# A pre-norm block of relative-position attention and routed experts: routed rows sent from a copy, stores issued by SyncE, the residual's bias added a batch ahead

## The chip, the core and the metric

The kernel runs on one core of a Trainium2 chip. The metric is the device time of one execution in microseconds (us). Engines are named as in the profile: PE is TensorE, DVE is VectorE, ACT is ScalarE, POOL is GpSimd (Pool), SP is SyncE, which computes nothing and issues transfers.

## The reference

The input x has 8 batches of 1024 tokens of 128 features. One layer computes, in float32:

```python
x = x + attention(layernorm(x))   # own layernorm again inside; 8 heads of 16
#   content = (q + u) k^T ; pos = rel_shift((q + v) (pe Wp)^T)
#   score = (content + pos) / sqrt(128); ctx = softmax(score) v; ctx Wo + bo
x = x + ffn(layernorm(x))
#   router: h = gelu(layernorm(x Wr1 + br1)); probabilities of 8 experts, the best 2, renormalised
#   each expert: (x1 * gelu(x2)) W2 + b2, with x1, x2 = split(x W1 + b1); weighted sum of the two
```

The relative shift makes the position term of score[q, k] one form below the diagonal and another above it, so a head's scores are made from two sets of stacked operands.

## The kernel before

The attention phase is one loop over the 8 batches, `b`, unrolled inside over 8 heads `h` and 9 units `u` (unit 0 makes the diagonal blocks of the upper form, units 1 to 8 the blocks of 128 keys, kb = u - 1). The expert phase follows it. The order of all work in the loop is written out by hand: tables such as `SCATTER_AT` hold pairs (h, u), and each engine does the piece at the end of its part of that unit. Engines run in program order, and semaphores are all that ties them.

In each unit PE makes a half of the scores of head h in `pB` (second pass, L639 to L645), and a piece of the first pass of head h + 2 in `pA` (L618 to L624), whose row maxima DVE takes (L1008, L1014); then again. ACT takes the exponential of `pB` into one of four buffers `prob` (L921, L923). Pool masks it: it sets one element to zero (L516), cuts the lower triangle (L518) and adds the upper form (L523), which releases `p_mask`; in unit 0 it masks the whole diagonal (L511). PE multiplies masked blocks with the values `vext` into `pC` (L657), in four column strips side by side, two kb at a time, in units 4, 6 and 8 and, for the last two, in unit 1 of the next head (`PAIRS_AT`). `vext` has 16 values and a one for each head, padded to VW = 32 columns.

Between these each engine has pieces for other batches. For the next batch: projections, the rotation of positions on Pool in eight pieces (`positions`, L429 to L441, at `POSITIONS_AT`), the split of the operands in a high and a low part (`high` on ACT, `low` on DVE, L995), and their stores to DRAM (`store`, L443, on Pool's queue, at `STORE_AT`, two transfers of 512 KB each call, ten in a batch). SP loads them as stacks of a head (`stack`, L270), three heads ahead; the first head of the next batch waits until all are stored (semaphore `stored`, in head 5). SP also moves the row of maxima of the next head (L277), swaps pairs of partitions (`swap`, L262) and shifts the values (`vsh` from `held`, L332). For the batch before: `xres`, loaded in head 0 (L312), gets its bias from Pool (`residual`, L455, at (1, 1)), then the attention's output from DVE (`final`, L1055), is stored, and the router works on it: statistics, `root` on Pool (L463, L465), rows (`router_apply`, L1078, L1081), hidden layer, logits, the two best, places (L1146 to L1170). Then Pool sends each row of 132 numbers to its two places in `routed_rows`, 16 indirect transfers of 128 rows each (`scatter`, L467, L476, at `SCATTER_AT`): the first in head 7, 15 in the next round's heads 0 to 2. `router_apply` waits for them before it overwrites `rows`.

After the loop the last batch has its own tail: the residual, 15 scatters left of the batch before, the two roots and 16 scatters on Pool; the output, the router and the table of tiles on DVE. Then come the experts, 72 tiles of 256 rows.

## Time and profile before

| | us |
|---|---|
| median of 3 runs (lowest, highest) | 1770.41 (1769.01, 1772.16) |
| the profiled execution | 1768.02 |
| its span, first to last instruction | 1766.4 |
| busy: PE, DVE, POOL, ACT | 1576.1, 1432.4, 1156.7, 1089.7 |

The profile is a page on one execution and a trace that can be asked. A row of instructions gives the line, the engine, the tile written and those read, the shape and the count, then busy time and the mean of one, then the engine's idle time just before them and what ended it. A row by stretch gives its ends and length in us, then the busy time (and the count) of PE, its weight loads (PEld), DVE, ACT and POOL, then the granted clock as a share of 2.4 GHz, the busy share of the 16 DMA engines and GB/s. A row of a timeline gives start and duration in us, and in brackets the idle time before it with its releaser. The time falls into a start (to 104 us), the eight batches (to 1280 us), a tail (to 1368 us) and the experts.

### The profile page before, as it was taken

To read this page: it belongs to the slowest core of one execution; us is meant where nothing else is said; L and a number is where in the kernel's file an instruction comes from. 1 tells how busy PE (TensorE), PEld (TensorE's weight loads), DVE (VectorE), ACT (ScalarE), POOL (GpSimd) and SP (SyncE) were. 2 spreads that over 40 slices of the span, in tenths; PEclk is the share of its full clock that TensorE was granted. 3 is DMA by queue.
4 is the path that set the end of the run, shared out by engine and by line. 5 is a ranking of instruction groups with operands and counts; after the bars stand their busy time and mean duration, and the time that the engine had idled before them with its cause. 6 is when DMAs were issued, how large, how long until landed. Compare 5 with 4: busy or idle time off the path is not lost. (4 is left out here: it accounts for less than half of the span.)

```text
span 1766.4 us, 50630 instructions
## 1 busy us (share of the span) xinstructions
PE 1576.1 (89%) x12534; PEld 1235.8 (70%) x12535; DVE 1432.4 (81%) x5423; ACT 1089.7 (62%) x2143; POOL 1156.7 (65%) x2139
## 2 busy tenths in 40 slices
PE   2699999999999999999999999999930999999997
PEld 1466776677677677667767667766720899999997
DVE  3479989998998898899899889889943677777775
ACT  2136676666767667666676766766710666676665
POOL 4149759858856865975885686597553366666655
PEclk8569999999999999999999999999965999999999
DMA  4534733733644463373364446337361233333333
GB/s 161 168 103 102 184 93 101 185 104 108 158 111 130 108 181 89 99 187 103 105 167 107 129 109 182 87 108 179 96 191 57 43 50 53 48 52 51 50 53 42
DMA packets 140439, 195.85 MB, mean 111 GB/s; under 512 B 27976, under 2 KB 102616, under 8 KB 140192
## 3 DMA queue, kind: packets, MB, share of 16 engines
q1 hardware_dynamic: 92608, 130.86, 27.0%
q0 software_dynamic: 47584, 62.19, 17.6%
q8 instruction: 94, 1.54, 0.4%
q14 instruction: 153, 1.25, 0.2%
HBM read 108.24 MB, written 75.27 MB: 104 GB/s over the span
## 5 line engine op out<-in xcount | busy, mean ns | idle before, releaser
L1008 DVE CUSTOM_DVE_ANT_0 junk<-pA,lmask 128x512 bf16<-128x512 f32 x1056 | 691.5, 682 | 106.8 <-PE pA L620 57.3
L921 ACT ACTIVATE prob<-pB 128x512 f32<-128x512 f32 x384 | 229.5, 598 | 189.9 <-PE pB L639 114.6
L1487 POOL DMA_INDIRECT out<-yb,dst x144 | 232.9, 1617 | 163.4 <-ACT yb L1561 87.2
L618 PE MATMUL pA<-K,QL 96*128 96x512 f32 (+3 forms) x792 | 286.2, 363 | 1.6 <-DVE acc L1008 1.6
L641 PE MATMUL pB<-QL,K 97*128 97x512 f32 (+3 forms) x768 | 281.3, 366 | 0.0
L639 PE MATMUL pB<-QU,K 97*128 97x512 f32 (+3 forms) x640 | 264.7, 414 | 0.9
L657 PE MATMUL pC<-prob,vext 128*32 128x256 f32 x3088 | 221.2, 387 | 26.7 <-POOL prob L523 26.7
L620 PE MATMUL pA<-K,QU 96*128 96x512 f32 (+3 forms) x660 | 233.7, 355 | 4.0 <-DVE acc L1008 3.8
L923 ACT ACTIVATE prob<-pB 128x512 f32<-128x512 f32 x384 | 227.8, 593 | 0.4
L523 POOL TENSOR_TENSOR prob<-prob,upper_diag 128x128 f32<-128x128 f32 x384 | 190.8, 497 | 32.3
L476 POOL DMA_INDIRECT routed_rows<-rows_r,idx x159 | 165.1, 1038 | 49.3 <-issue 26.5
L639 PEld LDWEIGHTS pB<-QU,K 97*128 97x128 f32 x640 | 121.6, 190 | 79.2 <-issue 50.8
L1599 DVE SCALAR_TENSOR_TENSOR g<-pLin,b_all,gl 128x256 f32<-128x256 f32 x292 | 126.2, 479 | 55.1 <-PE pLin L1510 33.5
L618 PEld LDWEIGHTS pA<-K,QL 96*128 96x128 f32 x792 | 154.8, 195 | 19.2 <-DVE acc L1008 11.4
L657 PEld LDWEIGHTS pC<-prob,vext 128*32 128x32 f32 x3088 | 84.0, 110 | 113.6 <-POOL prob L523 42.5
L641 PEld LDWEIGHTS pB<-QL,K 97*128 97x128 f32 x768 | 146.7, 191 | 14.7 <-ACT upper_diag L921 0.4
L1554 ACT ACTIVATE gl<-pGate,b_all 128x256 f32<-128x256 f32 x292 | 122.5, 471 | 46.8 <-issue 36.3
L620 PEld LDWEIGHTS pA<-K,QU 96*128 96x128 f32 x660 | 130.2, 197 | 19.2 <-DVE acc L1008 9.0
L1516 PE MATMUL pY<-w_all,g 128*128 x1152 | 140.4, 275 | 0.0
L511 POOL TENSOR_SCALAR_AFFINE_SELECT upper_diag<-upper_diag 128x1024 f32<-128x1024 f32 x64 | 70.2, 1097 | 100.7 <-ACT upper_diag L923 99.8
L1516 PEld LDWEIGHTS pY<-w_all,g 128*128 128x128 f32 x1152 | 134.2, 192 | 0.0
L921 ACT ACTIVATE b_all<-pB 128x512 f32<-128x512 f32 x128 | 76.5, 598 | 83.8 <-PE pB L639 57.0
(305 smaller groups left out, 3696.1 us busy)
## 6 DMA issues: line engine op xcount, KB each, us to landing
QL<-split_operands SPq DMA_DIRECT2D x67, 256.0 KB, 3.4
QU<-split_operands SPq DMA_DIRECT2D x67, 256.0 KB, 3.9
K<-split_operands SPq DMA_DIRECT2D x67, 256.0 KB, 4.6
xg<-routed_rows SPq DMA_DIRECT2D x76, 132.0 KB
QL<-split_operands SPq DMA_DIRECT2D x67, 128.0 KB, 3.4
QU<-split_operands SPq DMA_DIRECT2D x67, 128.0 KB, 3.7
K<-split_operands SPq DMA_DIRECT2D x67, 128.0 KB, 3.8
split_operands<-c_h POOLq DMA_DIRECT2D x16, 512.0 KB, 7.3
```

What stands on the lines that cost most here:

```text
L476: po.indirect_dma_start(dram["xs"], bass.IndirectOffsetOnAxis(idx[:, t, j:j + 1], 0), rows[:, t, :], None).then_inc(scattered, 16)
L523: po.tensor_tensor(p, p, upper_diag[h % 2][:, P * kb:P * kb + P], ALU.add).then_inc(p_mask, 1)
L618: mm = pe.matmul(dst[:, 0:low], QL[0:KROWS, s, q], K[0:KROWS, s, k0:k0 + low], start=True, stop=True)
L620: mm = pe.matmul(dst[:, low:HALF], QU[0:KROWS, s, q], K[0:KROWS, s, k0 + low:k0 + HALF], start=True, stop=True)
L639: mm = pe.matmul(pB[:, q0:q0 + up], K[0:r, s, k], QU[0:r, s, q0:q0 + up], start=True, stop=True)
L641: mm = pe.matmul(pB[:, q0 + up:q0 + HALF], K[0:r, s, k], QL[0:r, s, q0 + up:q0 + HALF], start=True, stop=True)
L657: mm = pe.matmul(pC[VW * strip:VW * strip + VW, :], vext[:, kb, h % H, :], prob[kb % RING][:, quarter * strip:quarter * strip + quarter], ...
L921: act.activation(p[:, 0:HALF], pB[:, 0:HALF], ACT.Exp, scale=SCALE).then_inc(p_exp, 1)
L923: act.activation(p[:, HALF:S], pB[:, HALF:S], ACT.Exp, scale=SCALE).then_inc(p_exp, 1)
L1008: v.tensor_tensor_reduce(junk[:, n % S1_BUFS, :], pA[n % S1_BUFS][:, :], lmask[:, at:at + HALF], 1.0, -3.0e38, ALU.add, ALU.max, acc[:, s, ...
L1487: po.indirect_dma_start(dram["out"], bass.IndirectOffsetOnAxis(dst[k][:, a:a + 1], 0), yb[k][:, a, :], None, compute_op=ALU.add).then_inc( ...
L1516: mm = pe.matmul(pY[k % 2][:, a, :], g[k % 2][:, c, P * a:P * a + P], keep["w2"][:, bass.ds(ex * F + c * E, E)], start=(c == 0), stop=(c = ...
```

## The change

It adds two tiles, `sent` and `sent_to`. At the end of head 7 SP waits until the places of the round are written and the scatters of this round have landed, and copies `rows` and `idx` into them; all 16 scatters of these go out in the next round, spread over heads 0, 1 and 3 to 6, and the last batch's go out of `rows` directly. `router_apply` waits for the copy where it waited for the scatters. The operands' stores are issued by SP, in heads 2, 3 and 4, each behind a row of maxima. `xres` is loaded in head 5 for the next round, and its bias is added in two halves in head 7; the first is loaded and done in the start. The rotation's pieces move to heads 1 and 2, the last two stay. `vext` is 17 wide, and so are the strips of `pC`; the product that once fills `pC` ahead of the loop takes its weights from `ident`. Counts of semaphores follow (`SET_R` 15, `res_done` 2 a batch).

```diff
-        vext = sb("vext", [P, NB, H, VW])
+        vext = sb("vext", [P, NB, H, D + 1])
...
+        sent, sent_to = sb("sent", [P, NB, ROW]), sb("sent_to", [P, NB, TOPK], U32)
...
-        POSITIONS_AT = ((2, 1), (2, 2), (2, 4), (2, 5), (2, 6), (2, 8), (5, 4), (5, 6))
+        POSITIONS_AT = ((1, 1), (1, 4), (1, 8), (2, 1), (2, 4), (2, 6), (5, 4), (5, 6))
...
-        RSTD_AT = ((3, 2), (3, 4), (3, 6), (3, 7), (4, 0), (4, 1), (4, 2))
-        RESIDUAL_AT, LAST_HEADS_AT, FIRST_HEADS_AT = (1, 1), (0, 6), (6, 4)
+        RSTD_AT = ((3, 2), (3, 4), (3, 5), (3, 7), (4, 0), (4, 1), (4, 2))
+        RESIDUAL_AT, LAST_HEADS_AT, FIRST_HEADS_AT = ((7, 1), (7, 4)), (0, 6), (6, 4)
...
-        SCATTER_AT = ((7, 6), (0, 2), (0, 3), (0, 4), (0, 5), (0, 6), (0, 8), (1, 0), (1, 2), (1, 3), (1, 4), (1, 5), (1, 6), (1, 7), (1, 8), (2, 0))
-        SAME_ROUND = sum(h == H - 1 for h, _ in SCATTER_AT)
+        SCATTER_AT = ((0, 1), (0, 4), (0, 6), (0, 8), (1, 6), (3, 1), (3, 6), (3, 8), (4, 4), (4, 6), (5, 1), (5, 8), (6, 1), (6, 4), (6, 6), (6, 8))
...
-        STORE_AT = {(3, 1): ("c", 0), (3, 3): ("c", 1), (3, 5): ("k", 0), (4, 5): ("gl", 0), (4, 6): ("gu", 0)}
+        STORE_AT = {2: ("c",), 3: ("k",), 4: ("gl", "gu")}
...
+            def store(nb, name):
+
+                highs, lows = known(sp, nb * HI_N + READY[name]), known(sp, nb * LOW_N + READY[name])
+                sp.wait_ge(set_dve, DVE_SET)
+                sp.wait_ge(hi_done, highs)
+                sp.wait_ge(low_done, lows)
+                for op, row in PLACES[name]:
+                    for low in range(2):
+                        sp.dma_start(stored_to(nb, op, low, row), parts[name][low][:, :].bitcast(F32)).then_inc(stored, 16)
...
+            sp.dma_start(xres[:, :, :], dram["x"][B - 1].rearrange("(t p) e -> p t e", p=P)).then_inc(d_res, 16)
...
-                        sp.wait_ge(d_x2, written)
-                        sp.dma_start(xres[:, :, :], dram["x"][bass.ds((b + B - 1) % B, 1)].rearrange("o (t p) e -> p (o t) e", p=P)).then_inc(d_res, 16)
...
+                    for name in STORE_AT.get(h, ()):
+                        store(b + 1, name)
...
+                        written, applied = known(sp, b * 16 + 32), known(sp, (b + 1) * RLN_N)
+                        sp.wait_ge(set_dve, DVE_SET)
+                        sp.wait_ge(d_x2, written)
+                        sp.wait_ge(r_ln, applied)
+                        sp.dma_start(xres[:, :, :], dram["x"][bass.ds(b, 1)].rearrange("o (t p) e -> p (o t) e", p=P)).then_inc(d_res, 16)
+                    if h + 1 == H:
+                        placed_rows, all_sent = known(sp, (b + 1) * RPOS_N), known(sp, (b + 1) * SCAT_N)
+                        sp.wait_ge(set_dve, DVE_SET)
+                        sp.wait_ge(r_pos, placed_rows)
+                        sp.wait_ge(scattered, all_sent)
+                        sp.dma_start(sent[:, :, :], rows[:, :, :]).then_inc(copied_out, 16)
+                        sp.dma_start(sent_to[:, :, :], idx[:, :, :]).then_inc(copied_out, 16)
...
-            sp.wait_ge(d_x2, (B + 1) * 16)
-            sp.dma_start(xres[:, :, :], dram["x"][B - 1].rearrange("(t p) e -> p t e", p=P)).then_inc(d_res, 16)
...
-            def store(nb, name, place):
-
-                highs, lows = known(po, nb * HI_N + READY[name]), known(po, nb * LOW_N + READY[name])
-                po.wait_ge(set_pool, POOL_SET)
-                po.wait_ge(hi_done, highs)
-                po.wait_ge(low_done, lows)
-                op, row = PLACES[name][place]
-                for low in range(2):
-                    po.dma_start(stored_to(nb, op, low, row), parts[name][low][:, :].bitcast(F32)).then_inc(stored, 16)
-
-            def residual(b):
-                po.wait_ge(d_res, b * 16 + 16)
-                po.tensor_tensor(xres[:, :, :], xres[:, :, :], bo_rows[:, :].unsqueeze(1).to_broadcast([P, NB, E]), ALU.add).then_inc(res_done, 1)
+            def residual(b, half):
+                if half == 0:
+                    po.wait_ge(d_res, b * 16 + 16)
+                four = slice(4 * half, 4 * half + 4)
+                po.tensor_tensor(xres[:, four, :], xres[:, four, :], bo_rows[:, :].unsqueeze(1).to_broadcast([P, 4, E]), ALU.add).then_inc(res_done, 1)
...
-                    placed_rows = known(po, (b + 1) * RPOS_N)
+                    copies = known(po, b * 32 + 32)
                     po.wait_ge(set_r, SET_R)
-                    po.wait_ge(r_pos, placed_rows)
-                elif n == SAME_ROUND:
-                    po.wait_ge(set_r, SET_R)
+                    po.wait_ge(copied_out, copies)
+                    po.sem_inc(going_out, 1)
+                po.indirect_dma_start(dram["xs"], bass.IndirectOffsetOnAxis(sent_to[:, t, j:j + 1], 0), sent[:, t, :], None).then_inc(scattered, 16)
...
+            po.wait_ge(m_done, 1)
+            for half in range(2):
+                residual(0, half)
...
-            residual(B)
-            for n in range(SAME_ROUND, NB * TOPK):
-                scatter(B - 1, n)
+            for n in range(NB * TOPK):
...
-                    mm = pe.matmul(pC[VW * strip:VW * strip + VW, :], vext[:, kb, h % H, :], prob[kb % RING][:, quarter * strip:quarter * strip + quarter],
+                    mm = pe.matmul(pC[VW * strip:VW * strip + D + 1, :], vext[:, kb, h % H, :], prob[kb % RING][:, quarter * strip:quarter * strip + quarter],
...
-                    v.wait_ge(scattered, b * SCAT_N + SCAT_N - 16 * SAME_ROUND)
+                    v.wait_ge(copied_out, b * 32 + 32)
...
```

## Rows read from the trace of the kernel before

**Rows 1.** Busy time by engine, stretches near heads 0 to 3 and 5, fourth batch.
```profile
547.00:565.00 18.00, 16.98 (x138) 12.24 (x137) 16.34 (x55) 12.64 (x25) 13.24 (x24) 1.00 0.35 100
565.00:585.00 20.00, 18.27 (x154) 13.17 (x154) 16.86 (x74) 11.88 (x23) 17.37 (x34) 1.00 0.33 98
585.00:603.00 18.00, 16.59 (x132) 11.30 (x132) 16.74 (x66) 12.04 (x23) 16.74 (x31) 1.00 0.36 107
603.00:623.00 20.00, 18.54 (x147) 13.22 (x148) 18.39 (x71) 13.72 (x27) 18.21 (x44) 1.00 0.77 184
...
641.00:658.00 17.00, 16.05 (x136) 11.43 (x136) 16.38 (x66) 12.80 (x24) 11.96 (x27) 1.00 0.53 151
```
**Rows 2.** The page's groups by cost: busy us, mean ns | idle before.
```profile
L657 PE MATMUL pC<-prob,vext 128*32 128x256 f32 x3088 | 221.2, 387 | 26.7 <-POOL prob L523 26.7
...
L476 POOL DMA_INDIRECT routed_rows<-rows_r,idx x159 | 165.1, 1038 | 49.3 <-issue 26.5
```
**Rows 3.** Timeline of PE in head 1 of the fourth batch.
```profile
574.86 0.64 PE L657 MATMUL pC<-prob,vext 128*32 128x256 f32 x8 [1.32 <-POOL prob L523]
```
**Rows 4.** Timeline of POOL ahead of that product.
```profile
571.00 2.99 POOL L455 TENSOR_TENSOR xres<-xres,bo_rows 128x1024 f32<-128x1024 f32 x1
...
574.35 0.46 POOL L523 TENSOR_TENSOR prob<-prob,upper_diag 128x128 f32<-128x128 f32 x1
```
**Rows 5.** Line 451, Pool's stores: ns min/median/max, first and last start.
```profile
L451 POOL DMA_DIRECT2D split_operands<-k_h x8: 657/657/657, 178.4 to 1206.8; - x8
```
**Rows 6.** Timeline of ACT, the first exponential of batches 2, 3 and 4.
```profile
253.75 0.60 ACT L921 ACTIVATE upper_diag<-pB 128x512 f32<-128x512 f32 x1 [0.19 <-PE pB L645]
400.12 0.60 ACT L921 ACTIVATE upper_diag<-pB 128x512 f32<-128x512 f32 x1 [0.19 <-PE pB L645]
547.19 0.60 ACT L921 ACTIVATE upper_diag<-pB 128x512 f32<-128x512 f32 x1 [0.19 <-PE pB L645]
```
**Rows 7.** Busy time by stretch, as rows 1: one with a lower clock.
```profile
416.00:424.00 8.00, 7.18 (x40) 5.18 (x44) 5.49 (x27) 2.97 (x6) 6.57 (x12) 0.57 0.82 237
```
**Rows 8.** The same for stores of Pool (343) and of SP (52).
```profile
343.00:350.00 7.00, 7.00 (x68) 5.23 (x67) 6.89 (x43) 4.80 (x11) 6.00 (x13) 1.00 0.91 211
52.00:58.00 6.00, 0.00 (x0) 0.00 (x0) 0.11 (x2) 0.00 (x0) 4.55 (x9) 0.50 0.51 210
```
**Rows 9.** Timelines of SP and PE, second batch; the page's landing of K's loads.
```profile
353.56 1.19 SPq L270 DMA_DIRECT2D QL<-split_operands  x2
...
364.21 0.27 PE L618 MATMUL pA<-K,QL 96*128 96x128 f32 x1
...
K<-split_operands SPq DMA_DIRECT2D x67, 256.0 KB, 4.6
```
**Rows 10.** DVE's last router step, Pool's mask of (0, 1), and vsh's landing (line 332).
```profile
392.32 0.17 DVE L1170 TENSOR_TENSOR rows_r<-gd,rows_r 128x8 f32<-128x8 f32 x1
...
403.57 0.46 POOL L523 TENSOR_TENSOR b_all<-b_all,upper_diag 128x128 f32<-128x128 f32 x1 [0.17 <-POOL b_all L518]
...
DMA to landing us min/median/max: 8.4/9.7/11.2
```
**Rows 11.** Weight loads of lines 657 and 598: ns min/median/max, first and last start.
```profile
L657 PEld LDWEIGHTS pC<-prob,vext x3088: 106/110/177, 108.2 to 1281.8; 128*32 128x32 f32 x193
...
L598 PEld LDWEIGHTS pM<-ident_f,mneg x41: 82/83/92, 98.0 to 1269.4; 128*8 128x8 f32 x41
```
**Rows 12.** Timeline of SP in the start: the swap.
```profile
27.71 5.27 SPq L262 DMA_DIRECT2D rq<-rp  x2
```
**Rows 13.** Timelines of POOL and DVE in the tail.
```profile
1281.64 2.36 POOL L455 TENSOR_TENSOR xres<-xres,bo_rows 128x1024 f32<-128x1024 f32 x1
...
1303.67 0.28 POOL L463 TENSOR_SCALAR rs_r<-mv_r 128x8 f32<-128x8 f32 x1
1304.04 1.68 POOL L465 TENSOR_TENSOR rs_r<-rs_r,mhalf 128x8 f32<-128x8 f32 x1
...
1306.50 0.17 DVE L1078 TENSOR_SCALAR rows_r<-rows_r 128x8 f32<-128x8 f32 x1 [9.72 <-DMA routed_rows<-rows_r,idx]
```

More of the change, by code:

```diff
@@ L211, in attention_phase @@
         RHID_N, RTOP_N, RTOP_DLT, RPOS_N = 3 * NB, 2 * NB + 5, 2 * NB + 1, 8
-        D_R, SET_R = 16 * 3, 14
+        D_R, SET_R = 16 * 3, 15
         M_PRO, M_N, W_N = 5, len(M_AT), len(W_AT)
@@ L303, in _ @@
             sp.sem_inc(moved, 16)
+            sp.sem_inc(copied_out, 32)
             with batches(nc, sp) as b:
@@ L306, in _ @@
                     if h == 0:
-                        written, normed = known(sp, b * 16 + 16), known(sp, (b + 2) * LN_N)
+                        normed = known(sp, (b + 2) * LN_N)
                         sp.wait_ge(set_dve, DVE_SET)
@@ L470, in scatter, with scatter_last @@
                 if n == 0:
-                    placed_rows = known(po, (b + 1) * RPOS_N)
+                    copies = known(po, b * 32 + 32)
                     po.wait_ge(set_r, SET_R)
-                    po.wait_ge(r_pos, placed_rows)
-                elif n == SAME_ROUND:
-                    po.wait_ge(set_r, SET_R)
+                    po.wait_ge(copied_out, copies)
+                    po.sem_inc(going_out, 1)
+                po.indirect_dma_start(dram["xs"], bass.IndirectOffsetOnAxis(sent_to[:, t, j:j + 1], 0), sent[:, t, :], None).then_inc(scattered, 16)
+            def scatter_last(n):
+                t, j = divmod(n, TOPK)
+                if n == 0:
+                    po.wait_ge(r_pos, (B + 1) * RPOS_N)
                 po.indirect_dma_start(dram["xs"], bass.IndirectOffsetOnAxis(idx[:, t, j:j + 1], 0), rows[:, t, :], None).then_inc(scattered, 16)
@@ L489, in _ @@
             po.memset(rows[:, :, :], 0.0).then_inc(set_r, 1)
+            po.memset(sent[:, :, :], 0.0).then_inc(set_r, 1)
             po.memset(both[:, :, :], 0.0).then_inc(set_r, 1)
@@ L523, in _ @@
                             po.tensor_tensor(p, p, upper_diag[h % 2][:, P * kb:P * kb + P], ALU.add).then_inc(p_mask, 1)
-                        if (h, u) == RESIDUAL_AT:
-                            residual(b)
+                        if (h, u) in RESIDUAL_AT:
+                            residual(b + 1, RESIDUAL_AT.index((h, u)))
                         if (h, u) in RSTD_AT:
@@ L529, in _ @@
                             positions(b + 1, POSITIONS_AT.index((h, u)))
-                        if (h, u) in STORE_AT:
-                            store(b + 1, *STORE_AT[h, u])
                         if (h, u) == ROOT_AT:
@@ L537, in _ @@
                             scatter(b, SCATTER_AT.index((h, u)))
-            residual(B)
-            for n in range(SAME_ROUND, NB * TOPK):
-                scatter(B - 1, n)
+            for n in range(NB * TOPK):
+                scatter(B, n)
             for i in range(2):
@@ L543, in _ @@
             for n in range(NB * TOPK):
-                scatter(B, n)
-            po.wait_ge(scattered, B * SCAT_N + (2 * NB * TOPK - SAME_ROUND) * 16)
+                scatter_last(n)
+            po.wait_ge(scattered, (B + 2) * SCAT_N)
         @block.tensor
@@ L770, in _ @@
             for j in range(0, P, VW):
-                pe.matmul(pC[j:j + VW, :], vext[:, 0, H - 1, :], prob[1][:, 0:S // STRIPS], start=True, stop=False, skip_group_check=True)
+                pe.matmul(pC[j:j + VW, :], ident[:, 0:VW], prob[1][:, 0:S // STRIPS], start=True, stop=False, skip_group_check=True)
             with batches(nc, pe, 0) as b:
@@ L1190, in small_piece @@
                     if which == 0:
-                        v.wait_ge(res_done, b + 1)
+                        v.wait_ge(res_done, 2 * b + 2)
                     final(which, src, done)
@@ L1232, in _ @@
             v.tensor_copy(mrow[0][:, :], pM[0:NB, 0:P]).then_inc(m_done, 1)
-            v.wait_ge(set_r, 12)
-            v.tensor_copy(idx[:, :, :].rearrange("p t j -> p (t j)"), lane[:, :]).then_inc(set_r, 1)
+            v.wait_ge(set_r, 13)
+            v.tensor_copy(sent_to[:, :, :].rearrange("p t j -> p (t j)"), lane[:, :]).then_inc(set_r, 1)
             v.wait_ge(d_r, D_R)
@@ L1280, in _ @@
                 normalized(B, i)
-            v.wait_ge(res_done, B + 1)
+            v.wait_ge(res_done, 2 * B + 2)
             v.memset(padrow, 0.0).then_inc(set_pad, 1)
```

6 lines of the change are left out of this document (4 added, 2 removed).

## The prediction

> **What bounds the kernel now.** I read the page's list of groups first, then the busy time by stage of one typical batch (the fourth, 547 to 694 us), then who waited for whom, then the order of Pool's and TensorE's work around each wait. Eight batches fill 104 to 1280 us, 146.4 us from one start to the next [rows 6]; before them stands a start that transfers bound, behind them a tail and 400 us of experts, which the change does not touch. TensorE is the bound in the batches: head 5 takes 17 us with 16.05 busy [rows 1]. In heads 0 to 3 it is not alone. Of 76 us there it is busy for 16.98 + 18.27 + 16.59 + 18.54 = 70.4, so 5.6 are idle; VectorE is busy for 16.34 + 16.86 + 16.74 + 18.39 = 68.3, a close second [rows 1]. The page says what TensorE lacks: its context product pC waits 26.7 us in all for L523, the last of Pool's three masking steps [rows 2]. The longest case in a batch is 1.32 us at 574.86 [rows 3]. Pool's own order tells why: at 571.00 it adds the output bias over 128x1024 in one piece of 2.99 us, and the mask that this product lacks starts only behind it, at 574.35 [rows 4]; all through heads 0 and 1 scatters stand between the masks in the same way. Pool is late and not overloaded: in head 5 it is busy for 11.96 of 17 us, in head 1 for 17.37 of 20 [rows 1].
>
> **The change part by part.**
>
> *Scatters, stores, bias and rotations leave heads 0 to 3.* A scatter costs Pool 1.04 us [rows 2] and some 0.2 ahead of it (of the 49.3 us idle over 159, 17.3 belong to one wait in the tail). Heads 0 and 1 held 14 of the 16. Now head 0 has four, head 1 one, head 2 none, and heads 3 to 6 the rest. Head 1 loses 2.99 + 7 x 1.2 = 11.4 us and gains three rotation pieces of about 1.3 (3.9); head 2 loses three of its six pieces and its scatter, some 5.1 us; head 3 loses three pairs of stores, four us at 0.67 or so for each of six [rows 5] and gains three scatters (3.6). In heads 4 to 6 stand about 8 scatters, 9.8 us, where two pairs of stores leave and Pool has been idle for 5 us in head 5 alone [rows 1]. Large extras now stand in units next to each other only around the root of head 2. TensorE takes kb 0 and 1 in unit 4, two units behind the mask, so a delay of one extra is covered. The 26.7 us can go. What is late next is VectorE: with TensorE busy throughout, head 5 leaves it 17 - 16.38 = 0.6 us idle [rows 1]; heads 0 to 3 can then not fall below 68.3 + 4 x 0.6 = 70.7 us in VectorE's account, while TensorE's is 76 - 26.7 / 8 = 72.7. So in total all of it can come. Head by head VectorE gives less: head 2 can go from 18 to 16.74 + 0.6 = 17.3, and not by the 1.3 us that a wait costs, and with three banks of pA between the two engines gaps do not move freely. I take three quarters, **-20.0 us**, bounds -10 (VectorE takes most) and -26.7.
>
> *The clock.* TensorE's granted clock is 1.00 in nearly all of the batches, and fell to the lower of its two levels, 1.2 GHz, in five short stretches; in the one at 416 us the mean is 0.57 [rows 7]. Each begins where TensorE waits for Pool. Without the wait they should go. The batch with the stretch at 416 took 547.19 - 400.12 = 147.07, the one before it, without, 146.37 [rows 6]: 0.7 x 5 = 3.5 at most, nothing at least; I take **-1.5**.
>
> *Stores from SP.* For Pool -6.6 us a batch, counted above. For SP ten transfers of 512 KB more, behind each row of maxima. Rates: while SP stored such operands in the start, 210 GB/s; while Pool did, 211 [rows 8]. So 2.5 us each on either queue. gl and gu go out once split, in head 4's units 3 and 4, where Pool issued them in units 5 and 6, so they land no later. The loads that wait for them stay behind the row of head 6 and went out at 353.56; three tiles at 1.19 us of issue and a landing 4.6 us after the last make 361.8, and TensorE wants them at 364.21 [rows 9]. Cost 0, with 2.4 us of cover and what the earlier issue adds; behind that each us late is a us a batch. The same rows show a difference: SP's stores held 0.51 of the 16 DMA engines busy, Pool's 0.91 [rows 8]. The Trainium skill, "DMA: Bandwidth & Descriptors", section "Why a DMA increments its semaphore by 16 and not by 1", has a queue of SP spread a copy over the largest number up to 16 that divides its slowest dimension; that is the 8 heads here, and the trace agrees with its 0.51. By the rate of the rows it adds nothing; it is why the rival on SP has the chance it has.
>
> *The copy and the waits on it.* SP copies 0.54 MB of rows and the indices once VectorE has written the last column, 392.49 in the second batch; the next round's first scatter follows the mask of head 0's unit 1, which ends at 404.03 [rows 10]. The nearest copy between SBUF tiles, vsh from held, lands 8.4 to 11.2 us after its issue, beside Pool's stores [rows 10]: cover of 0.3 us at the worst, 1.8 at the median, and behind it the two units of slack of the masks, which queue behind Pool's wait. Cost 0, bounds 0 and 1 us a batch. VectorE now waits for the copy instead of the scatters; both are long past at (3,0).
>
> *The bias a batch ahead.* Its 2.99 us becomes two halves in head 7, where Pool has room; its load moves to head 5. Cost 0.
>
> *Contexts 17 wide instead of 32.* A weight load of 32 columns shows 110 ns, one of 8 shows 83 [rows 11]; 17 would be near 93. But four strips stream side by side (221.2 us busy for 3088 matmuls is 72 ns each, where one lasts 387 [rows 2]), and loads run under them, so only the first load of each of 256 runs of two products can be seen: 256 x 17 ns = 4.4 us less at most. On the other side nothing in the trace has strips 17 wide; if each product of eight matmuls, 0.57 us, took a tenth longer, 512 x 0.06 = 30 us more. I take 0, since the streaming of 256 columns, which stays, covers the loads. The Trainium skill, "TensorE: Matmul & The Clock Gate", section "LDWEIGHTS (loading the stationary operand)", has the load go by columns over 1.2 GHz, an estimate of 12.5 ns less for 15 columns; the rows' slope gives 17.
>
> *The start.* One more load of 512 KB (the first xres) goes ahead of the swap, which was issued at 27.71 [rows 12] and whose landing releases the rotations, the last stores and so the first pass. Its bytes take 2.5 us at the 210 GB/s of rows 8, if none of it fits beside the others, and nothing if all does. **+1.5**, since the queue is full there: the swap's own issue took 5.27 us [rows 12]. The first bias add on Pool lies in the wait for the statistics that follow.
>
> *The tail.* Pool ended its last mask at 1281.7, did the bias in 2.36, then 15 scatters at (1303.67 - 1284.00) / 15 = 1.31 us, and only then the root of the last batch, whose statistics had kept VectorE waiting since 1306.50 - 9.72 = 1296.8; VectorE waited on, past the root's end at 1305.72, until 1306.50 for the last scatter to land, before it could overwrite the rows [rows 13]. Now there are 16 scatters and no bias, so the root starts 2.36 - 1.31 = 1.0 us earlier, and rows may be written as it ends, 0.8 us earlier still. **-1.8**, bounds -1.0 and -3. The last 16 scatters stay as they are.
>
> **Sum.** The profiled execution took 1768.0 us with a span of 1766.4; 1768.0 - 20.0 - 1.5 + 1.5 - 1.8 = 1746.2. The median shown is 2.4 us above that execution, so 1748.6 for a median.
>
> **The rivals.**
> 1. *VectorE becomes the bound at once.* For it: 68.3 of 76 us busy, and three banks of pA between it and TensorE. Against: it has gaps of its own right after each wait for Pool. Heads 0 to 3 keep VectorE's waits and only half of the 20 comes, 1759. Chance 0.14.
> 2. *It doesn't do what it says.* The scatters in heads 3 to 6 delay masks there as they did in heads 0 and 1, where TensorE had no idle time to lose. Gain under 3.5 us, about 1769. Against: 5 of 17 us free. 0.06.
> 3. *Slower: SP's stores block the loads behind them.* Place: four stores of gl and gu from head 4's middle, on half of the DMA engines, ahead of the maxima of head 6 and the first operands of the next batch on one queue. They must land by 353.56 + 2.4 = 356 or so; each us beyond is one us in each of 8 batches, and the change is slower from 359 on, where 22 / 8 = 2.7 us a batch eat the gain. At 360, 32 us against 22, it gives 1781. For it: the 0.51; against: their 10 us of transfer start two units earlier than before. 0.08.
> 4. *Narrow strips lose part of their overlap*, the 30 us bound above: 1779, slower. Loads of 8 columns that cost less than those of 32 [rows 11] speak against it. 0.04.
> 5. *The copy lands late.* From 6 us beyond the mask of (0,1) on, masks stall TensorE; at 10 us, 4 x 8 = 32 us lost, 1781. 0.03.
>
> **How the numbers follow.** The forecast, 1748.6, has 0.62, with 1740 to 1757 as its own range; 0.03 is left for a larger gain. I set the range from 1737 (all of Pool's waits, the clock and half the narrow loads) to 1762 (rival 1 with the start's upper bound). A measurement of this kernel tells about 0.2%, 3.5 us, from no change. Faster: 0.62 + 0.14 + 0.03 = 0.79; same 0.06 (rival 2); slower 0.08 + 0.04 + 0.03 = 0.15.
>
> **What the profile after would show.** Right: the wait of pC for L523 under 5 us in all; batches of 143 to 144 us; granted clock 1.00 through them; VectorE's waits for pA in heads 0 to 2 gone; the root of the tail near 21 us behind the last mask; no wait of PE for QL, QU or K. Wrong: waits of pA for VectorE in the place of pC's (rival 1); pC waiting in heads 4 to 6 (2); TensorE waiting for QL, QU or K at a head's start (3); more than 72 ns of busy time for each pC matmul (4); Pool idle at (0,1) for a DMA (5).

## The result, and the profile after

The changed kernel takes 1721.98 us (median of 4 runs, 1720.53 to 1724.11); the kernel before, on the same chip, 1769.71 (1766.31 to 1772.16). The ratio is 0.9733, 95% interval 0.9713 to 0.9752: 48 us less by the medians, where 22 were forecast and the stated range ended at 1737. The profiled execution took 1724.11 us with a span of 1722.4. By stages (before, after): start 103.8, 105.7; the eight batches up to the last unit's exp 1175.7, 1133.7; from there to the experts' first row blocks 86.3, 81.6; the experts 400.7, 401.4. The batches brought 42 of the 44 us by which the two profiled executions differ.

Groups of instructions of the kernel after (columns as in [rows 2]; L680 is the context product, L657 before; L643 a product of the first pass; L491 the scatter out of the copy):

```profile
L643 PE MATMUL pA<-K,QU 96*128 96x512 f32 (+3 forms) x660 | 232.4, 353 | 5.2 <-DVE acc L1031 4.7
L491 POOL DMA_INDIRECT routed_rows<-sent,sent_to x144 | 148.1, 1029 | 30.4 <-issue 27.6
L680 PE MATMUL pC<-prob,vext 128*17 128x256 f32 x3088 | 215.2, 381 | 0.0
L680 PEld LDWEIGHTS pC<-prob,vext 128*17 128x17 f32 x3088 | 77.7, 97 | 81.8 <-issue 22.5
```

The 26.7 us for which pC waited for Pool's mask in [rows 2] are 0.0. Busy time by stage (columns as in [rows 1]): three whole batches, the second to the fourth, then heads 0 to 3 and head 5 of the fourth:

```profile
251.05:392.61 141.56, 139.17 (x1159) 101.52 (x1159) 131.93 (x549) 100.00 (x190) 100.82 (x229) 1.00 0.47 136
392.61:534.19 141.58, 139.25 (x1159) 101.50 (x1159) 132.04 (x548) 100.02 (x190) 100.87 (x229) 1.00 0.48 136
534.19:675.75 141.56, 139.23 (x1159) 101.51 (x1159) 132.01 (x549) 100.07 (x190) 100.79 (x229) 1.00 0.48 136
...
534.24:550.95 16.71, 16.68 (x137) 12.11 (x136) 15.14 (x46) 12.63 (x25) 11.99 (x27) 1.00 0.33 90
550.95:569.62 18.67, 17.93 (x153) 13.19 (x152) 17.42 (x82) 12.01 (x24) 12.43 (x30) 1.00 0.35 97
569.62:586.25 16.63, 16.55 (x137) 12.01 (x136) 16.60 (x71) 12.19 (x24) 13.63 (x27) 1.00 0.60 163
586.25:604.11 17.86, 17.61 (x143) 12.49 (x143) 16.82 (x65) 13.66 (x27) 13.74 (x35) 1.00 0.72 218
...
622.17:639.79 17.62, 16.65 (x141) 11.86 (x140) 17.02 (x71) 12.87 (x25) 13.53 (x29) 1.00 0.52 153
```

From the second on a batch lasts 141.56 us, against 146.4 to 147.9 (two of them in [rows 6]), and each is like the next; the first takes 145.3, 150.0 before. In the fourth batch heads 0 to 3 take 69.87 us instead of 75.72 (the 76 of [rows 1], cut at the heads' ends). TensorE's idle time there is 1.1 us instead of 5.6. Heads 4 to 6 are as before, head 7 is 0.3 us longer. And VectorE is busy for 65.98 us in heads 0 to 3 where it was for 68.09, though it runs the same instructions (4366 in the eight batches of either kernel). One of them, the low part of an operand in head 2, with Pool's operation beside it, before:

```profile
592.06 1.28 POOL L432 TENSOR_TENSOR g_lo<-rp,cos_lo 128x512 f32<-128x512 f32 x1
592.26 1.63 DVE L995 TENSOR_TENSOR c_l<-qu,c_h 128x512 fp32r<-128x512 f32 x1
```

and after:

```profile
576.61 1.16 POOL L549 TENSOR_TENSOR prob<-prob,upper_diag 128x128 f32<-128x128 f32 x1
576.77 0.67 DVE L1018 TENSOR_TENSOR c_l<-qu,c_h 128x512 fp32r<-128x512 f32 x1
```

Beside a rotation piece VectorE needs 1.63 us for it, otherwise 0.67. In the second case Pool is held instead: its mask takes 1.16 us where most take 0.46.

What the wait of pC leaves over is in the clock. The stretches of the batches in which the granted clock was at its lower level (0.50 of full, 1.2 GHz), of the kernel before, the first being the end of the start's:

```profile
103.79:109.63 5.84, 5.84 (x30) 3.95 (x29) 2.88 (x9) 2.91 (x5) 1.85 (x3) 0.50 0.77 224
123.28:130.11 6.83, 6.83 (x32) 4.96 (x36) 4.31 (x24) 2.44 (x5) 5.58 (x10) 0.50 0.84 256
416.83:423.66 6.83, 6.83 (x32) 4.99 (x36) 4.32 (x24) 2.42 (x5) 5.58 (x10) 0.50 0.85 256
741.10:744.51 3.41, 3.41 (x16) 2.27 (x14) 2.02 (x10) 1.17 (x2) 3.24 (x8) 0.50 0.00 0
870.80:874.21 3.41, 3.41 (x15) 3.12 (x14) 1.67 (x6) 1.19 (x2) 2.94 (x9) 0.50 0.15 44
1164.35:1167.76 3.41, 3.41 (x15) 3.11 (x14) 1.67 (x6) 1.19 (x2) 2.94 (x9) 0.50 0.14 44
```

and the only two of the kernel after:

```profile
105.72:110.41 4.69, 4.69 (x18) 3.50 (x21) 2.28 (x8) 2.43 (x5) 1.10 (x1) 0.50 0.61 173
202.60:206.01 3.41, 3.41 (x18) 2.62 (x22) 2.40 (x8) 1.61 (x3) 0.61 (x3) 0.50 0.68 145
```

29.7 us at half speed became 8.1. At full speed that work takes half the time, so 14.9 and 4.1 us are lost in them, 10.8 less.

This gives a sum that I tested on every kernel run since. I take the time of the eight batches (start of the first unit's exp to start of the last unit's), subtract TensorE's idle time (that stretch less its busy time, from the view of busy time by stage), and half of the time at half speed. If idle and clock are all that differs, what is left is the same for all kernels. (Batches less idle is TensorE's busy time, so the test is whether busy time differs by the clock alone.)

| kernel | batches | idle | half of the half-speed time | left |
|---|---|---|---|---|
| before | 1175.7 | 45.6 | 14.9 | 1115.2 |
| after | 1133.7 | 18.9 | 4.1 | 1110.7 |
| before, 17 columns | 1172.8 | 51.4 | 9.2 | 1112.3 |
| before, stores on SP | 1172.7 | 42.5 | 16.8 | 1113.5 |
| before, 17 columns and copy | 1173.9 | 41.0 | 18.3 | 1114.6 |
| the same, stores on SP | 1143.0 | 29.3 | 3.0 | 1110.7 |
| after, scatters in heads 0 and 1 | 1197.6 | 42.7 | 47.4 | 1107.4 |
| after, stores on Pool | 1165.9 | 32.2 | 19.8 | 1113.9 |
| after, bias at (1,1) | 1135.1 | 23.0 | 2.4 | 1109.6 |
| after, a rotation at (2,8) | 1140.8 | 24.5 | 3.2 | 1113.0 |
| after, Pool delayed | 1155.7 | 32.7 | 12.8 | 1110.2 |
| after, hidden rows earlier | 1147.9 | 20.1 | 16.8 | 1111.0 |
| after, hidden rows earlier, xres load later | 1149.3 | 20.0 | 18.3 | 1110.9 |
| after, consumers later, xres load later | 1130.1 | 15.4 | 2.5 | 1112.2 |
| after, xres load later | 1131.9 | 18.7 | 2.5 | 1110.7 |

The batches vary by 67 us, the last column by 8. So of the 42 us, 26.7 are idle time (as much as [rows 2] showed for pC, the other waits balance), 10.8 clock, and 4.5 lie in what the view counts as busy, which is less than the last column varies.

### The profile page after: what moved, and what is told of

It reads as the page before. It is cut to its first block and busy times, and to the rows that moved or that the text cites. A ratio compares the mean times of both kernels' runs of the same rounds, so it can differ in the third digit from the quotient of the medians.

```text
span 1722.4 us, 50666 instructions
## 1 busy us (share of the span) xinstructions
PE 1561.8 (91%) x12534; PEld 1222.0 (71%) x12535; DVE 1426.2 (83%) x5423; ACT 1090.2 (63%) x2143; POOL 1108.4 (64%) x2070
## 5 line engine op out<-in xcount | busy, mean ns | idle before, releaser
L643 PE MATMUL pA<-K,QU 96*128 96x512 f32 (+3 forms) x660 | 232.4, 353 | 5.2 <-DVE acc L1031 4.7
L549 POOL TENSOR_TENSOR prob<-prob,upper_diag 128x128 f32<-128x128 f32 x384 | 196.8, 512 | 32.1
L680 PE MATMUL pC<-prob,vext 128*17 128x256 f32 x3088 | 215.2, 381 | 0.0
L491 POOL DMA_INDIRECT routed_rows<-sent,sent_to x144 | 148.1, 1029 | 30.4 <-issue 27.6
L542 POOL MEMSET prob<- 1x1 f32 x384 | 34.3, 89 | 175.4 <-ACT prob L946 171.2
L643 PEld LDWEIGHTS pA<-K,QU 96*128 96x128 f32 x660 | 128.8, 195 | 22.7 <-DVE acc L1031 12.5
L680 PEld LDWEIGHTS pC<-prob,vext 128*17 128x17 f32 x3088 | 77.7, 97 | 81.8 <-issue 22.5
L1037 DVE CUSTOM_DVE_ANT_0 junk<-pA,umask 128x128 bf16<-128x128 f32 x528 | 117.4, 285 | 13.5 <-PE pA L647 13.3
```

The costliest lines, as they stand in the source:

```text
L549: po.tensor_tensor(p, p, upper_diag[h % 2][:, P * kb:P * kb + P], ALU.add).then_inc(p_mask, 1)
L643: mm = pe.matmul(dst[:, low:HALF], QU[0:KROWS, s, q], K[0:KROWS, s, k0 + low:k0 + HALF], start=True, stop=True)
L680: mm = pe.matmul(pC[VW * strip:VW * strip + D + 1, :], vext[:, kb, h % H, :], prob[kb % RING][:, quarter * strip:quarter * strip + quarter ...
```

## Experiments

Theory A at the outset: Pool's late masks are the whole matter, and cost TensorE more than the idle column says, since the modelled end of a matmul (381 ns on the mean) reaches past the next start. The rivals are named in the expectations. Each kernel's ratio is to the kernel before on its own chip (1767.5 to 1768.1 us there). Distances to the kernel after are between medians taken on different chips; by the ratios they come out up to 2.5 us otherwise.

### Bias back at (1,1)

```diff
-        RESIDUAL_AT, LAST_HEADS_AT, FIRST_HEADS_AT = ((7, 1), (7, 4)), (0, 6), (6, 4)
+        RESIDUAL_AT, LAST_HEADS_AT, FIRST_HEADS_AT = (1, 1), (0, 6), (6, 4)
...
-                            residual(b + 1, RESIDUAL_AT.index((h, u)))
+                            residual(b)
```

> The changed kernel, with one part undone: the bias is added in one piece of some 3 us at (1,1) of its own batch, and in the tail ahead of the scatters; its load stays where the change put it. Theory A (a late mask costs TensorE more than the profile's idle column shows, because the modelled end of a waiting matmul, 379 ns, reaches over the 215 ns to the next start): the piece now stands with a rotation piece of 1.3 us behind one mask, so head 1 gets longer by 1.2 to 1.8 us in each batch, 10 to 14 us in all, and the tail by 1.3 us: 1733 to 1738 us. The idle that pC shows for the mask is then well under the loss, 5 to 9 us in all. Rival B (the idle column is the whole loss, the rest of the gain came from elsewhere): loss and idle agree within 1 us. Rival C (Pool has room enough now for a single piece): no more than 1725.

Measured: 1726.4 us, ratio 0.9764 [0.9742, 0.9787], 4 us over the kernel after (5 by the ratios). Head 1 is 0.6 us longer, the idle shown for pC is 0.2 us in all, and the root of the tail is 1.7 us later. The forecast of 1733 to 1738 missed, and so, by a little, did rival C (no more than 1725): of what took 2.99 us in [rows 4] nearly everything fits now. What head 1 loses shows as waits for VectorE's first pass (10.8 us in all, 6.0 after), not for the mask. In the kernel before it was the scatters around the piece that made it matter: with them spread and the bias still whole at (1,1), pC waits for nothing in heads 0 to 2, with the stores on Pool or on SP (the last two runs of "One part alone").

### Scatters back in heads 0 and 1

```diff
-SCATTER_AT = ((0, 1), (0, 4), (0, 6), (0, 8), (1, 6), (3, 1), (3, 6), (3, 8), (4, 4), ...)
+SCATTER_AT = ((0, 1), (0, 2), (0, 3), (0, 4), (0, 5), (0, 6), (0, 8), (1, 0), (1, 2), ...)
```

> The changed kernel, with the scatters put back into heads 0 and 1 (16 of them, two in three units), though still out of the copy. Theory A: the masks of heads 0 and 1 are late again, 2.0 to 2.7 us a batch lost, 16 to 22 us in all: 1738 to 1744. The idle of pC for the mask shows only some two thirds of it. Rival B: loss equals the idle shown. Rival C (it was the stores and the bias that did it, Pool can carry the scatters alone): under 1728.

Measured: 1788.0 us, ratio 1.0120 [1.0094, 1.0146]. The loss is 66 us, three to four times the forecast, and the kernel is slower than the one before. Heads 0 to 2 of its fourth batch, then two stretches in them:

```profile
555.16:573.26 18.10, 17.06 (x137) 12.08 (x136) 16.47 (x55) 12.64 (x25) 14.39 (x26) 0.99 0.38 102
573.26:594.13 20.87, 20.69 (x153) 15.00 (x153) 16.83 (x72) 12.12 (x24) 17.62 (x35) 0.84 0.32 90
594.13:615.85 21.72, 19.65 (x137) 13.69 (x137) 16.35 (x70) 12.41 (x24) 17.33 (x33) 0.84 0.62 189
...
572.92:579.75 6.83, 6.83 (x37) 4.56 (x36) 4.21 (x17) 3.02 (x6) 6.15 (x13) 0.50 0.83 235
603.64:610.47 6.83, 6.35 (x27) 4.41 (x31) 2.49 (x9) 2.48 (x5) 3.91 (x11) 0.50 0.50 148
```

In head 1 TensorE is busy for 20.69 of 20.87 us, at a mean clock of 0.84: a reader of idle time alone would find nothing wrong there. Such stretches of 6.83 us stand twice in five of the batches, 13 in all; each begins within 2 us of a wait for the mask. By the sum, 24 us of the loss are idle time and 43 the clock. A late mask is paid twice where such a stretch follows.

### Stores back on Pool

```diff
-                    for name in STORE_AT.get(h, ()):
-                        store(b + 1, name)
+                        if (h, u) in STORE_AT:
+                            store(b + 1, *STORE_AT[h, u])
```

> The changed kernel with the stores of the operands issued by Pool again, in the five places of the kernel before (three in head 3, two in head 4). Theory A: head 3 had 0.82 us of late masks a batch before, with stores and no scatters there; now three scatters stand there too, so head 3 loses 0.8 to 1.5 us a batch: 1728 to 1734. Rival C (Pool has room for them): under 1725. Rival E (the stores from SP cost something that goes with them): faster than 1720.

Measured: 1758.4 us, ratio 0.9942 [0.9920, 0.9963]: 36 us lost, again far above the forecast. Heads 3 to 5 of the fourth batch:

```profile
595.89:615.39 19.50, 17.79 (x143) 12.23 (x143) 17.14 (x65) 13.63 (x27) 15.59 (x34) 1.00 0.88 211
615.39:633.98 18.59, 18.23 (x155) 13.41 (x155) 16.59 (x67) 11.49 (x23) 16.53 (x38) 1.00 0.64 153
633.98:652.89 18.91, 17.05 (x141) 11.92 (x141) 18.34 (x70) 12.83 (x25) 14.73 (x34) 1.00 0.70 183
```

The loss isn't at the masks alone (pC waits 4.8 us in all). Head 5, without a store in it, takes 18.91 us here and 19.8 to 21.9 in the other seven batches, which have a half-speed stretch in it, against 17.6: Pool comes 1.5 us late to the root at (4,8), VectorE later to the hidden rows, and TensorE's wait for them grows from 0.97 to 1.48 us a batch. VectorE is busy for 19.4 us more in the batches, with the same work. By the sum 13 us of the loss are idle time and 16 the clock.

### One part alone, from the kernel before

> The kernel before, with only the stationary operand of the context product narrowed to 17 columns. Theory A: nothing on its own, since the masks set the pace in heads 0 to 3 and the streaming covers the loads elsewhere: within 3 us of the kernel before. Rival D (narrow loads give time in each run of products): 4 us or more faster, and then the matmul starts of pC in heads 4 to 7 stand 2.72 us apart per head and the heads are shorter too.

Measured: 1764.0 us, ratio 0.9983 [0.9972, 0.9993]. The starts of pC's matmuls stand 2.72 us apart in a head, 2.77 before, and heads 4 to 7 are 0.15 us a batch shorter, 1.2 in all. Small, and real. In the kernel after the width can't be put back: with 32 columns the copy's tiles leave 384 bytes of SBUF a partition where 512 are needed, so the width is measured from this side alone.

> The kernel before, with only the stores of the operands moved to SP's queue. Theory A (with the scatters in heads 0 and 1 the stores are not what fills Pool; they cost head 3 its 0.8 us of late masks a batch and little else): 6 to 12 us faster, with heads 0 to 2 as before. Rival F (the stores cost 36 us wherever they stand, as in the changed kernel): 30 us or more faster. Rival G (stores on SP delay loads behind them): slower than before, with TensorE waiting for QL, QU or K.

Measured: 1765.0 us, ratio 0.9976 [0.9964, 0.9987]. That is less than the 6 to 12 us of theory A: head 3 gets 0.2 us shorter, not 0.8. TensorE waits for no operand (rival G is out). Of stores that cost 36 us in the changed kernel, 3 to 4 are to be had here (rival F is out).

> The kernel before, with the 17 columns (the copy of the rows finds room only so), the copy, and the scatters spread over heads 0 to 6; stores stay on Pool, bias and rotations in heads 1 and 2. Theory H (the parts depend on each other: Pool has no room for both the scatters and the stores in heads 3 to 5): heads 0 and 1 get 2 to 3 us a batch shorter, heads 3 to 5 get 3 us longer with a half-speed stretch in head 5: within 10 us of the kernel before. Rival I (the scatters alone bring the gain): 25 us or more faster.

```diff
+                        sp.dma_start(sent[:, :, :], rows[:, :, :]).then_inc(copied_out, 16)
...
-SCATTER_AT = ((7, 6), (0, 2), (0, 3), (0, 4), (0, 5), (0, 6), (0, 8), (1, 0), ...)
+SCATTER_AT = ((0, 1), (0, 4), (0, 6), (0, 8), (1, 6), (3, 1), (3, 6), (3, 8), (4, 4), ...)
```

Measured: 1769.1 us, ratio 1.0005 [0.9995, 1.0015]. As theory H has it: in heads 0 to 2 all of pC's waits are gone (heads of 16.72, 18.66, 16.63 us, as in the changed kernel), and heads 3 to 5 take 20.2, 18.6 and 20.2 us on the mean instead of 19.3, 18.1 and 17.6. Late masks are the smaller part of that: pC waits 5.6 us in all, but pA waits 18.3 us for VectorE (6.8 before) and pM 11.9 for its hidden rows (7.5 before), and seven half-speed stretches stand in heads 3 and 5.

> As the run with the copy, and the stores on SP as well: what lacks to the changed kernel is the bias a batch ahead and the rotations spread. Theory H: nearly the whole gain is there; head 1 keeps 0.7 us for the bias, head 2 up to 1.3 for its six rotation pieces: 1728 to 1740. Rival J (bias and rotations are a third of the gain or more): above 1740.

Measured: 1733.9 us, ratio 0.9811 [0.9795, 0.9827]. The stores alone give 3, copy and spread scatters alone (with the columns) nothing, both 34: some 70% of the gain is this pair. Of the 12 us that lack, head 3 has more than all: 19.45 us against 17.89, 12.5 in the eight batches, with no wait of pC, but 1.4 us of waits for VectorE's first pass. Against that head 7 is 0.34 us shorter here, 2.7 in all, without the bias in it.

### A rotation beside VectorE's rows

```diff
-POSITIONS_AT = ((1, 1), (1, 4), (1, 8), (2, 1), (2, 4), (2, 6), (5, 4), (5, 6))
+POSITIONS_AT = ((1, 1), (1, 4), (1, 8), (2, 1), (2, 4), (2, 8), (5, 4), (5, 6))
```

The reason stands in the order of operations about (3,0). Kernel before with columns, copy and SP stores, VectorE and then Pool (start, length, engine, line):

```profile
588.92 2.54 DVE L1097 SCALAR_TENSOR_TENSOR rows_r<-xres,mv_r,rs_r 128x128 f32<-128x128 f32 x2
...
588.93 1.28 POOL L462 TENSOR_TENSOR g_lo<-g_lo,t 128x512 f32<-128x512 f32 x1
590.17 1.15 POOL L529 TENSOR_SCALAR_AFFINE_SELECT upper_diag<-upper_diag 128x1024 f32<-128x1024 f32 x1
```

and the same place in the kernel after:

```profile
588.71 0.63 DVE L1104 SCALAR_TENSOR_TENSOR rows_r<-xres,mv_r,rs_r 128x128 f32<-128x128 f32 x2
...
587.67 1.10 POOL L537 TENSOR_SCALAR_AFFINE_SELECT upper_diag<-upper_diag 128x1024 f32<-128x1024 f32 x1
```

Two pieces of rows_r take 0.63 us behind Pool's operation and 2.54 beside two of them: each of those two ends within 0.2 us of Pool's. VectorE's first pass, with scores from PSUM as one input, keeps its 0.68 us beside the same operations. The Trainium skill, "SBUF — State Buffer", section "Who interferes with whom", says that a VectorE instruction with two inputs in SBUF and a GpSimd instruction that reads SBUF exclude each other for the length of the one that came first; the trace agrees, with 1.45 and 1.17 us for the two pieces where one alone takes 0.34. Which came first it can't tell for the first piece, whose start lies 0.01 us ahead of Pool's. In the kernel after another instruction is held at this place, `rows_r<-rows_r` (L1101), a tensor_scalar with one input: 0.85 us for 0.17, until Pool's L537 ends.

> The changed kernel with one rotation piece put back from (2,6) to (2,8). In the trace of the run with copy and SP stores, VectorE's rows_r pieces at (3,0) and (3,1) took 1.45 and 1.17 us instead of 0.34, each ending as Pool's rotation piece and Pool's masking of upper_diag ended beside it, and head 3 took 19.45 us instead of 17.89. Theory K (VectorE is held by a Pool operation beside it, and the rotation's place is what counts): head 3 gets 1.0 to 1.6 us longer in each batch, without any wait of pC for the mask: 1730 to 1736 us. Rival L (head 3 gained by the number of pieces in head 2, three instead of six): within 3 us of the changed kernel.

Measured: 1731.5 us, ratio 0.9786 [0.9766, 0.9805]. One operation of 1.28 us, two units later, costs 9.5 us by the medians, 7.1 between the two profiled executions: head 3 takes 18.89 us instead of 17.89, pC waits for nothing, and VectorE's busy time in the batches goes from 1054.1 to 1061.9 us. Theory K holds.

### A dose of Pool time

```diff
+                        DOSE = {(0, 2): 8, (6, 2): 12, (7, 2): 16}
+                        for i in range(DOSE.get((h, u), 0)):
...
+                            po.tensor_tensor(spare[:, :], spare[:, :], spare[:, :], ALU.add).then_inc(dosed, 1)
```

> The changed kernel with idle work for Pool of known size added behind the mask of unit 2: 8, 12 and 16 operations over 128x64 in heads 0, 6 and 7, by 0.38 us each an estimated 3, 4.6 and 6 us. It measures what a late mask costs. Theory A (a wait of TensorE hides some 0.16 us behind the modelled end of the matmul before it, and short waits wholly): the head gets longer by more than the idle shown for pC, by a quarter to a half; head 0 loses under 0.5 us a batch, head 6 0.5 to 1.5, head 7 1.5 to 3. In all 20 to 35 us. Rival B: loss and idle agree.

Measured: 1742.9 us, ratio 0.9849 [0.9825, 0.9873]. From the first operation's start to the last one's end the doses were 3.7 to 4.1, 4.5 and 5.9 us; an operation takes 0.29 to 0.44 us by its place. In the third to seventh batches head 6 loses nothing, head 0 0.41 us with 0.37 idle for pC, head 7 1.48 with 1.53 to 1.58. The wait in head 7 of the fourth batch:

```profile
681.72 0.63 PE L687 MATMUL pC<-prob,vext 128*17 128x256 f32 x8 [1.38 <-POOL prob L551]
```

Loss and idle agree, so my first theory, that the idle column hides a part, falls. The rest of the 21 us came as clock: the three batches with a half-speed stretch (the first, second and last) lost 1.9, 3.1 and 4.3 us more than the others.

### The wait for the hidden rows, twice

```diff
-NORM_HIDDEN_AT = ((5, 1), (5, 2))
+NORM_HIDDEN_AT = ((5, 0), (5, 1))
```

> The changed kernel with VectorE's two pieces of the router's hidden rows one unit earlier, at (5,0) and (5,1): the only wait of TensorE of size that is left, 0.97 us a batch at (5,3), is for them. Theory M (it is on the path): it goes and head 5 gets 0.6 to 1.0 us shorter: 1712 to 1717, with the half-speed stretch at 202 us gone too. Rival N (VectorE gives it back as a wait of pA in head 5): within 2 us of the changed kernel.

Measured: 1735.8 us, ratio 0.9814 [0.9797, 0.9832]: 14 us slower than the kernel after. The wait for hr is gone and another is there. TensorE in head 5 of the fourth batch (in brackets idle before, releaser), then the clock right behind:

```profile
628.68 0.50 PE L643 MATMUL pA<-K,QU 96*128 96x512 f32 x1 [0.22 <-DVE acc L1031]
...
630.96 0.50 PE L643 MATMUL pA<-K,QU 96*128 96x512 f32 x1 [0.94 <-DVE acc L1031]
631.30 0.75 PE L733 MATMUL pM<-ident_f,hr 128*128 128x128 f32 x4
...
631.61:635.02 3.41, 3.41 (x21) 2.27 (x23) 3.15 (x12) 2.15 (x4) 0.79 (x4) 0.50 0.33 79
```

Both forecasts missed. Idle time is 1.3 us more in all, next to nothing; but a half-speed stretch of 3.41 us stands at (5,3) of all eight batches, 12.7 us by the sum. The kernel after has its one wait of 0.97 there, and a stretch in one batch of eight.

The same with that load later (edit below) and `(1, 8)` of the rotations at `(1, 7)`:

> The run before it, and two more edits: the first load of xres and its bias come behind the first operand stacks, not ahead of the swap, and the rotation piece of (1,8) goes to (1,7), away from VectorE's dsup, which took 0.83 us more a batch beside it. Expected: the start 1.5 to 2.5 us shorter, head 1 or 2 up to 0.5 us a batch shorter: 1708 to 1714. If the load had been free in the start, no more than the run before it.

Measured: 1733.9 us, ratio 0.9795 [0.9772, 0.9818]; head 5 is as in the run before it, and moving the piece of (1,8) changes no head, though VectorE is busy for 4.8 us less in the batches: held time off TensorE's path costs nothing here. The start took 103.8 us, no less than the 103.2 of the run before it. The forecast of 1708 to 1714 stood on that run's gain, which didn't come.

The consumers one unit later instead, and the load later:

> The changed kernel with the first load of xres and its bias behind the first operand stacks, and with the consumers of the router's hidden rows one unit later instead of the producers one earlier: the fold, its copy, cube, tanh, gelu and the context that follows move from (5,3) to (5,8) by one unit each. The sum by stages as the runs so far give it (batches = 1111 us of work + TensorE's idle time + half of the half-speed time): the wait of 0.97 us a batch at (5,3) goes, 7.8 us, if nothing of its size comes up behind it at the logits of (6,0), and with it the half-speed stretch in the first batch: 1710 to 1714. Rival O (the wait reappears for pA or the logits, as when the producers were moved): 1720 or more, with a half-speed stretch in every batch if the new wait is 0.9 us or longer and stands close behind another.

```diff
-                "row 5": ((4, 1),), ... "fold": ((5, 3),), "context 4": ((5, 5),), "logits": ((6, 0),),
+                "row 5": ((4, 1),), ... "fold": ((5, 4),), "context 4": ((5, 6),), "logits": ((6, 0),),
...
-        CUBE_AT, TANH_AT, GELU_AT, TOP_AT, EXP_AT = (5, 5), (5, 6), (5, 7), ...
+        CUBE_AT, TANH_AT, GELU_AT, TOP_AT, EXP_AT = (5, 6), (5, 7), (5, 8), ...
```

Measured: 1718.5 us, ratio 0.9719 [0.9705, 0.9733]. The 7.8 us for hr went, 3.8 for pA came: VectorE is busy for 16.57 of head 5's 17.37 us. No stretch at half speed begins in the batches; the start's reaches 4.9 us into them. The forecast of 1710 to 1714 missed, and rival O (1720 or more) isn't reached either. It is the fastest kernel here, 2 us under the one with only the load moved; its interval overlaps with the changed kernel's, so that it beats that one isn't shown, only that it beats the kernel before.

The move of the load, which both this kernel and the next have:

```diff
-            sp.dma_start(xres[:, :, :], ...).then_inc(d_res, 16)
             swap(0)
...
                 stack(0, h)
+            sp.dma_start(xres[:, :, :], ...).then_inc(d_res, 16)
```

> The changed kernel with only the first load of xres and its bias moved behind the first operand stacks. Profiled starts with the load ahead of the swap took 103.2 to 106.3 us (seven kernels), those without it 101.6 to 103.8 (five). If the load costs the start 2 us, 1719 to 1721; if the spread is noise of the start's transfers, 1721 to 1723.

Measured: 1720.7 us, ratio 0.9732 [0.9719, 0.9746]. Starts of the profiled executions with the load ahead of the swap: 103.2 to 106.3 us, mean 105.5 (seven); without it 101.6 to 104.1, mean 103.2 (eight). By these means 2.3 us of the start belong to the load, though the two groups overlap. The execution times don't decide it: the median is 1.3 us under that of the kernel after, which ran on another chip, and the ratios to the kernel before, 0.9732 and 0.9733, are equal, each within some 3.5 us.

## Where the prediction was right and where wrong

*Pool's waits, -20.0 taken of 26.7.* The mechanism was right; all of it came. I held back a quarter because VectorE could not go below 68.3 us of busy time in heads 0 to 3. That step fails: it took VectorE's busy time as work. Part of it was VectorE held by Pool's operations, and went with them: 68.09 us before and 65.98 after for the same instructions, and 69.87 for the heads, under the floor of 70.7 that I had worked out. In head 2, for which I had worked out 17.3, VectorE's operations together ran 1.9 us longer than the same ones take at their fastest (1.0 of it the one of 1.63 us above), and now run 0.15 longer; the head takes 16.63. Rival 1 rests on the same step; the waits for pA that it names did not come (6.8 us in the batches before, 6.0 after).

*The clock, -1.5, bounds 0 and -3.5.* It is -10.8, the largest error. That is the step that failed most: I priced a stretch as the difference of two neighbouring batches, 0.7 us [rows 6]. But there a stretch took the place of a wait. The sixth batch, with one at (1,4), shows no wait of pC in head 2, where those without have 1.3 us, and lasts 146.42 us, as long as the second, which has none; the third, with the stretch of [rows 7] in head 0, has none of the 1.3 us in head 1 and half of those in head 2. Each of the two costs hides the other while both stand. Two runs from the kernel before show the trade: 17 columns alone took 5.7 us off the clock's share and put 5.8 on the idle time, the stores alone took 3.1 off the idle time and put 1.9 on the clock's share. With both gone their sum comes. Alone, a stretch of 3.41 us costs half its length: head 5 of the first batch after takes 19.23 us, 17.59 in the others. Half of the 23.9 us of the five stretches like that of [rows 7] would have given 12.

*A rest of 4.5 us* has no term of mine. It lies in time counted as busy. The run with 17 columns alone has 2.9 us less in the last column of the table than the kernel before, of which 1.2 are seen in heads 4 to 7; but kernels that share these columns differ there by up to 7 us. Short waits that fit under a modelled matmul end were my guess, which the doses of Pool time don't bear out. The cause of this part stays open.

*Stores from SP, 0, copy, 0.* Right in these places: no wait for QL, QU or K, none of Pool for a copy (its waits ahead of scatters are "issue"). What I didn't see is that spread scatters without this edit bring nothing. Rival 2 comes near it, scatters that delay work in heads 3 to 6, though by VectorE's waits more than by masks; the stores' leaving is what keeps it away. I added the parts' costs; these two depend on each other.

*Bias, 0.* Right to some 3 us. Its new place isn't free: the second half stands beside VectorE's `rows_r<-ex,gd` (L1191), which takes 1.27 us for 0.17, and head 7 lasts 17.25 us, against 16.93 with the bias at (1,1). *17 columns, 0*: -1.2 for the loads, within the bounds; rival 4 is out (69.7 ns busy for each matmul, 72 before).

*Rotations* were counted as Pool time alone. The place of one of them beside `rows_r` is worth 7 to 10 us.

*Start, +1.5*: +1.9 in the two profiles, 2.3 by means. *Tail, -1.8*: -4.6. The root started 21.5 us behind the last mask (22.0 before, 21 forecast), and from its start to the last scatter's it is 1.1 us less, 1.6 together, close to my term. The other 3 us, which I had at nothing ("the last 16 scatters stay as they are"), lie at the end of the scatters; last scatter and first operation behind it, kernel after:

```profile
1313.96 0.96 POOL L498 DMA_INDIRECT routed_rows<-rows_r,idx  x1 [0.30 <-issue]
1320.64 0.14 POOL L1513 IOTA pad_slot<- 128x8 f32 x1 [5.72 <-POOLq L73]
```

and the kernel after with the stores on Pool:

```profile
1346.31 0.96 POOL L506 DMA_INDIRECT routed_rows<-rows_r,idx  x1 [0.30 <-issue]
1355.38 0.14 POOL L1523 IOTA pad_slot<- 128x8 f32 x1 [8.11 <-POOLq L73]
```

This wait is 8.1 to 8.8 us in the four kernels whose Pool issues the stores, long done by then, and 5.7 to 6.0 in the eleven whose Pool issues only scatters. The run that only moves the stores shows it alone: 8.75 us in the kernel before, 5.68 in that run.

Sum for the profiled executions: -26.7 - 10.8 - 4.5 + 1.9 - 4.6 + 0.7 (experts) = -44.0; forecast -21.8. Of the signs that I gave, pC's wait, the root, and no wait for QL, QU or K came as said. The batches are 2 us shorter than the 143 to 144 given, one stretch at the lower clock stands in them, and VectorE's waits for pA in heads 0 to 2 of the fourth batch are not gone but halved (2.6 us, 4.9 before).

## What to carry to other kernels

Before you sum the gains of a scheduling change, list every stretch at the lower clock with the wait that it starts at, and price the wait with its stretch at half its length: two limits that cover each other look cheap one at a time. Read the second engine's busy time for operations that last longer beside a third engine; such a floor moves when the third engine's work does. When an engine is short of time in one place, test the edits that free it together as well as alone.

## What the runs showed of the hardware

- Every stretch at the lower clock in the batches (3.41, 6.83 or 13.65 us) began within some 2 us of a wait of TensorE, of 0.6 to 1.6 us, in one case of 0.4. The reverse doesn't hold: of the 27 waits of 0.8 us or more in the batches before, 22 stand neither in nor ahead of one; 16 of 0.9 to 1.2 us in the kernel with columns, copy and SP stores brought none; one of 0.94 to 1.07 us in the kernel after brought one in 1 batch of 8, two of 0.22 and 0.94 us some 2.3 us apart in 8 of 8.
- VectorE operations with two inputs in SBUF were held until Pool's operation beside them ended (1.45 us for 0.34, 1.63 for 0.67), and one with a single input too (0.85 for 0.17); the first pass, which reads PSUM, was not (0.65 to 0.70 us beside the same operations). Pool was held in turn (1.16 us for 0.46). Over the batches VectorE's busy time varied from 1048.8 to 1073.9 us among kernels with the same count of VectorE instructions.
- With the same last 16 scatters, Pool's queue took 8.1 to 8.8 us to come free where it had also issued plain stores, 5.7 to 6.0 where it had not. Why isn't shown.
